# Expert stage of a graph and mixture-of-experts kernel: row-number copies on VectorE, scatter waits by loaded numbers, fetch distance of two

## What is computed

```python
gate_scores = x @ Wg + bg
_, idx = jax.lax.top_k(gate_scores, K)                    # K = 2 of E = 8 experts
mask = jax.nn.one_hot(idx, E, dtype=x.dtype).sum(axis=-2)
h = jax.nn.gelu(jnp.einsum('td,edh->teh', xf, W1) + b1[None], approximate=False)   # 256 -> 512
y = jnp.einsum('teh,ehd->ted', h, W2) + b2[None]                                     # 512 -> 256
out = jnp.einsum('ted,te->td', y, mf)
```

## Time and profile before

| | us |
|---|---|
| median of 3 runs | 177.0 (176.54 to 177.05) |
| profiled execution, its own time | 177.12 |
| its span in the trace | 175.3 |
| PE busy | 143.2 (82% of the span) |
| POOL busy | 74.8 (43%) |
| DVE busy | 89.3 (51%) |
| ACT busy | 65.3 (37%) |
| granted TensorE clock, mean | 0.989 of full speed |

### The profile page before, as it was taken

One profiled execution on the slowest core, in us unless ns is written; L12 is line 12 of the kernel. 1 busy time (PEld: TensorE's weight loads), 2 busy tenths in 40 slices (PEclk: granted clock), 3 DMA queues, 4 the chain that ended last, 5 costly groups with the idle time before them and its releaser, 6 DMA issues.

```text
span 175.3 us, 3032 instructions
## 1 busy us (share of the span) xinstructions
PE 143.2 (82%) x971; PEld 120.1 (69%) x972; DVE 89.3 (51%) x235; ACT 65.3 (37%) x183; POOL 74.8 (43%) x99
## 2 busy tenths in 40 slices
PE   1353384999999999989999948989999999999710
PEld 1332272998899899979999936857666666766600
DVE  6689999778799650305036885622222222223100
ACT  8333876467312140315030480323443333334200
POOL 6804930000499049950000200075555666663662
PEclk9999999999999999999999999999999999999995
DMA  4629999990000789400000432014244333332332
GB/s 146 194 28 310 369 366 366 368 316 12 6 0 4 204 299 327 142 4 0 0 0 4 134 128 97 0 60 90 30 71 79 64 62 60 60 64 30 60 60 30
DMA packets 16055, 20.33 MB, mean 116 GB/s; under 512 B 1754, under 2 KB 12388, under 8 KB 15908
## 3 DMA queue, kind: packets, MB, share of 16 engines
q1 hardware_dynamic: 13492, 16.54, 29.0%
q0 software_dynamic: 2544, 3.54, 12.0%
HBM read 16.81 MB, written 3.26 MB: 115 GB/s over the span
## 4 chain that ended last, share of the span: by engine, by line
PE 63%; DMA 11%; DVE 11%; issue 5%; POOL 3%; ACT 2%; POOLq 1%; SPq 1%; ACTq 0%; DVEq 0%
PE cnt_ps L1658 9%; PE bank L1639 6%; PE bank L1509 6%; DMA x_sb<-in_x 5%; PE cnt_ps L1509 4%; PE g_ps L1639 4%; PE g_ps L1344 3%; PE g_ps L1345 3%; PE g_ps L1346 3%; PE cnt_ps L1652 3%; DMA out_rows<-y_sb,row_put 2%; DMA out_rows<-y_sb,row_of 2%; DVE hot_lo L971 2%; PE cnt_ps L1344 2%; DMA xg<-x_rows,row_of 2%
## 5 line engine op out<-in xcount | busy, mean ns | idle before, releaser
L1658 PE MATMUL cnt_ps<-w_sb,h_t 128*128 x104 | 24.7, 380 | 1.1 <-ACT h_t L886 1.1
L1658 PEld LDWEIGHTS cnt_ps<-w_sb,h_t 128*128 128x128 f32 x104 | 18.8, 190 | 3.8 <-issue 1.8
L652 POOL DMA_INDIRECT out_rows<-y_sb,row_of x10 | 15.9, 1591 | 12.5 <-DMA out_rows<-y_sb,row_of 9.9
L646 POOL DMA_INDIRECT xg<-x_rows,row_of x12 | 12.1, 1005 | 18.6 <-DVE row_of L1313 15.2
L1400 PE MATMUL bank<-hot_key,hot_lo 125*128 125x45 bf16 (+4 forms) x80 | 8.3, 243 | 11.6 <-DVE hot_key L974 7.5
L1400 PEld LDWEIGHTS bank<-hot_key,hot_lo 125*128 125x128 bf16 x80 | 5.3, 123 | 13.9 <-DVE hot_key L974 13.0
L971 DVE TENSOR_TENSOR hot_lo<-iota_lo,edge_rel 125x1024 bf16<-125x1024 int16 x20 | 13.9, 697 | 1.6 <-PE g_ps L1400 1.5
L1282 DVE TENSOR_TENSOR y_sb<-cnt_ps,b_bc 128x256 f32<-128x256 f32 x13 | 5.5, 424 | 17.6 <-PE cnt_ps L1658 17.6
L1639 PE MATMUL bank<-w_sb,xt 128*128 x28 | 13.4, 600 | 0.7 <-ACT xt L890 0.5
L1278 DVE TENSOR_TENSOR h_pre<-bank,b_bc 128x512 f32<-128x512 f32 x7 | 4.8, 692 | 13.8 <-PE bank L1639 13.8
L882 ACT ACTIVATE h_act<-h_pre 128x512 f32<-128x512 f32 x13 | 8.2, 630 | 9.3 <-DVE h_pre L1278 9.3
(11 more groups left out here) (299 smaller groups left out, 405.0 us busy)
## 6 DMA issues: line engine op xcount, KB each, us to landing
w_sb<-in_L_ffn_W SPq DMA_DIRECT2D x16, 512.0 KB, 10.2
b_bc<-in_L_ffn_b SPq DMA_DIRECT2D x8, 256.0 KB, 4.8
w_stage<-in_L_gnn_W SPq DMA_DIRECT2D x3, 512.0 KB, 6.2
w_stage<-in_L_gnn_Wf SPq DMA_DIRECT2D x4, 256.0 KB, 7.5
b_bc<-in_L_ffn_b SPq DMA_DIRECT2D x1, 1024.0 KB, 8.4
x_rows<-x_f SPq DMA_DIRECT2D x1, 640.0 KB, 3.3
x_sb<-in_x SPq DMA_DIRECT2D x1, 512.0 KB
out_rows<-x_sb SPq DMA_DIRECT2D x1, 512.0 KB
```

The lines of the kernel that those rows point to most:

```text
L646: pool.indirect_dma_start(out=xg[:, b, :], out_offset=None, in_=x2_rows, in_offset=bass.IndirectOffsetOnAxis(ap=rows, axis=0)).then_inc(x_ ...
L652: pool.indirect_dma_start(out=out, out_offset=bass.IndirectOffsetOnAxis(ap=rows, axis=0), in_=y_sb[:, b, :], in_offset=None, compute_op=AL ...
L1658: last = pe.matmul(bank[3][:, 0:D], h_t[:, k, :], w2_sb[:, ds(e, 1), k, :], start=k == 0, stop=k == HC - 1)
```

## The change

- `AHEAD` is 4 instead of 5: POOL gathers two tiles instead of three before the first scatter, and in step s the tile s + 4, which PE consumes in its step s + 2. Step 9 now has a gather too (tile 13).
- `scattered` becomes two semaphores, for even and for odd tiles. Scatter s waits for its own parity (scatter s - 2 landed) and for the other parity up to a number. That number counts scatter s - 1 in if the two tiles have different experts, and leaves it out if they have the same one: an expert's tiles hold different nodes.
- DVE works the numbers out (`same_expert`, `turn_i`), and POOL loads seven of them into registers before the first gather, for tiles 3 to 9; each late tile loads its own. Tiles 1 and 2 wait for constants.
- `row_put` and `row_get` are copied by DVE, ahead of the late tile's `add_b2`, and no longer by POOL.
- SP, at the end, waits for two semaphores instead of one.

```diff
-AHEAD = 5
+AHEAD = 4
@@ gpsimd
+            pool.iota(turn_base[:].rearrange("p (k h) -> p k h", h=2), pattern=[[16, SLOT_TILES // 2], [16, 2]], base=0,
+                      channel_multiplier=0, **small).then_inc(turn_base_ready, 1)
+            pool.wait_ge(turn_ready, 1)
+            turns = [other_turn(pool, v) for v in range(3, FIXED)]
             pool.wait_ge(rows_ready, 1)
             pool.wait_ge(x2_stored, 32)
...
             for s in range(FIXED):
-                if s:
-                    pool.wait_ge(scattered, s * 16)
+                if s >= 2:
+                    pool.wait_ge(scattered[s % 2], s // 2 * 16)
+                if s in (1, 2):
+                    pool.wait_ge(scattered[1 - s % 2], 16)
+                elif s:
+                    pool.wait_ge(scattered[1 - s % 2], turns[s - 3])
                 pool.wait_ge(y_ready, s + 1)
-                scatter(s % 4, row_of[:, s:s + 1])
+                scatter(s % 2, s % 4, row_of[:, s:s + 1])
                 if AHEAD + s < FIXED + 4:
...
+            def late_scatter(s, h, n_late, n_pairs):
+                turn = other_turn(pool, s)
                 pool.wait_ge(put_taken, n_late)
                 pool.wait_ge(y_ready, s + 1)
-                pool.wait_ge(scattered, s * 16)
+                pool.wait_ge(scattered[h], n_pairs * 16 + FIXED // 2 * 16)
+                pool.wait_ge(scattered[1 - h], turn)
                 pool.sem_inc(pool_turn, 1)
...
-                    next_put(s + 1, 1 - h)
-                    pool.wait_ge(x_t_done, s + 1)
-                    pool.tensor_copy(row_get[:, h:h + 1], row_of[:, ds(s + 4, 1)]).then_inc(get_taken, 1)
@@ vector
+            dve.tensor_tensor(same_expert[:, 1:], owner[:, 1:SLOT_TILES], owner[:, 0:SLOT_TILES - 1], ALU.is_equal)\
+                .then_inc(same_ready, 1)
+            dve.wait_ge(turn_base_ready, 1)
+            dve.wait_ge(same_ready, 1)
+            dve.scalar_tensor_tensor(turn_i[:, 1:], same_expert[:, 1:], -16.0, turn_base[:, 1:], ALU.mult, ALU.add)\
+                .then_inc(turn_ready, 1)
...
-                    dve.wait_ge(scattered, s * 16 - 16)
+                    dve.wait_ge(scattered[h], p * 16 + FIXED // 2 * 16)
+                    dve.tensor_copy(row_put[:, h:h + 1], row_of[:, ds(s, 1)]).then_inc(put_taken, 1)
+                    dve.wait_ge(x_t_done, s + 1)
+                    dve.tensor_copy(row_get[:, h:h + 1], row_of[:, ds(s + 4, 1)]).then_inc(get_taken, 1)
                     add_b2(s, 2 + h, e_down)
```

More of the change, by code:

```diff
@@ L231, in build @@
         pairs_i = sb("pairs_i", [1, 2], i32, ffn)
+        turn_base = sb("turn_base", [1, SLOT_TILES], f32, ffn)
+        same_expert = sb("same_expert", [1, SLOT_TILES], f32, ffn)
+        turn_i = sb("turn_i", [1, SLOT_TILES], i32, ffn)
         iota_p = sb("iota_p", [P, P], f32, ffn)
@@ L350, in build @@
         x_t_done = sem("x_t_done")
-        scattered = sem("scattered")
+        scattered = [sem(f"scattered{h}") for h in range(2)]
+        turn_base_ready = sem("turn_base_ready")
+        same_ready = sem("same_ready")
+        turn_ready = sem("turn_ready")
         xt_ready = sem("xt_ready")
@@ L419, in up_bank, with other_turn @@
             return (bank[1], g_ps[0])[s % 2]
+        def other_turn(eng, s):
+            return eng.value_load(turn_i[0:1, ds(s, 1)], min_val=16, max_val=16 * SLOT_TILES)
         def expert_of(eng, s):
@@ L519, in _ @@
                 sp.wait_ge(x_got[h], more * 16 + 16)
-            sp.wait_ge(scattered, more * 32 + is_odd * 16 + FIXED * 16)
+            sp.wait_ge(scattered[0], more * 16 + is_odd * 16 + FIXED // 2 * 16)
+            sp.sem_inc(all_scattered, 1)
+            sp.wait_ge(scattered[1], more * 16 + FIXED // 2 * 16)
             sp.sem_inc(all_scattered, 1)
@@ L648, in gather, with scatter @@
                     in_offset=bass.IndirectOffsetOnAxis(ap=rows, axis=0)).then_inc(x_got[b], 16)
-            def scatter(b, rows):
+            def scatter(h, b, rows):
                 pool.indirect_dma_start(
                     out=out, out_offset=bass.IndirectOffsetOnAxis(ap=rows, axis=0),
-                    in_=y_sb[:, b, :], in_offset=None, compute_op=ALU.add).then_inc(scattered, 16)
+                    in_=y_sb[:, b, :], in_offset=None, compute_op=ALU.add).then_inc(scattered[h], 16)
             for s in range(2, AHEAD):
@@ L668, in _ @@
             is_odd = odd_tile(pool)
-            def next_put(s, h):
-                pool.tensor_copy(row_put[:, h:h + 1], row_of[:, ds(s, 1)]).then_inc(put_taken, 1)
-            def late_scatter(s, h, n_late):
+            def late_scatter(s, h, n_late, n_pairs):
+                turn = other_turn(pool, s)
                 pool.wait_ge(put_taken, n_late)
                 pool.wait_ge(y_ready, s + 1)
-                pool.wait_ge(scattered, s * 16)
+                pool.wait_ge(scattered[h], n_pairs * 16 + FIXED // 2 * 16)
+                pool.wait_ge(scattered[1 - h], turn)
                 pool.sem_inc(pool_turn, 1)
-                scatter(2 + h, row_put[:, h:h + 1])
-            pool.tensor_copy(row_put[:, 0:1], row_of[:, FIXED:FIXED + 1]).then_inc(put_taken, 1)
+                scatter(h, 2 + h, row_put[:, h:h + 1])
             with pool.Fori(0, more) as p:
@@ L684, in _ @@
                     s = p * 2 + (FIXED + h)
-                    late_scatter(s, h, p * 2 + (h + 1))
-                    next_put(s + 1, 1 - h)
-                    pool.wait_ge(x_t_done, s + 1)
-                    pool.tensor_copy(row_get[:, h:h + 1], row_of[:, ds(s + 4, 1)]).then_inc(get_taken, 1)
+                    late_scatter(s, h, p * 2 + (h + 1), p)
                     pool.wait_ge(get_taken, p * 2 + (h + 1))
@@ L692, in _ @@
             with pool.If(is_odd > 0):
-                late_scatter(more * 2 + FIXED, 0, more * 2 + 1)
+                late_scatter(more * 2 + FIXED, 0, more * 2 + 1, more)
         @block.scalar
@@ L1320, in _ @@
                 if s >= 4:
-                    dve.wait_ge(scattered, 16 * (s - 3))
+                    dve.wait_ge(scattered[s % 2], 16 * (s // 2 - 1))
                 add_b2(s, s % 4, e_of[s])
@@ L1334, in _ @@
                 s = more * 2 + FIXED
-                dve.wait_ge(scattered, s * 16 - 16)
+                dve.wait_ge(scattered[0], more * 16 + FIXED // 2 * 16)
+                dve.tensor_copy(row_put[:, 0:1], row_of[:, ds(s, 1)]).then_inc(put_taken, 1)
                 add_b2(s, 2, expert_of(dve, s))
```

## The result

The changed kernel takes 179.91 us (median of five executions, 178.01 to 182.86), the kernel before 177.05 in the same comparison: a ratio of 1.0129, with a 95% interval from 1.0085 to 1.0172. The ratio is taken over executions within 1.5% of the fastest of their kernel; it is not the quotient of the two medians. It is slower, as forecast, but 1.9 us above the predicted 178.0 and 1.1 us outside the range. Four of those five executions had a mean granted clock of 0.955 to 0.967, at which before takes some 2 us more as well (the table under c2_after); compared again on two chips, the change read 1.0100 (1.0046 to 1.0155) and 1.0088 (1.0048 to 1.0128).

The account below looks back on a forecast made before the run. The prediction took gapless PE (steps 1 to 9) as the bound, with scatters bound by y and late ones by landings. PE's 1.76 us delay minus 0.80 gained at the end gave +0.96, so 178.0 us; range 176.4 to 178.8.

Parts of the forecast that it names:

- X(s): Start on PE of the transposes of fetched rows in step s, those of tile s + 2; X(11) predicted 1.76 us late.
- T(12): Start on POOL of scatter 12, the last; predicted at 171.18 us against 170.22 before.
- the prediction's own recurrence: Step-by-step starts on PE and POOL, each the later of normal pace (4.10 us a step) and landing or fetch bound.
- The landing wait costs 0.8 us where it stands ahead of the scatter.: POOL, fixed part, where the expert changes: the wait costs 0.80 us instead of under 0.4.
- The rival by which it stays cheap: POOL's landing wait costs no more ahead of the scatter than inside it; 176.4 us, chance 0.17.
- Its size: At expert changes, scatter follows scatter by at least 3.74 + 0.80 = 4.54 us on POOL, against a step of 4.10.
- the sum: Whole kernel: PE 1.76 us late, less 0.80 gained at the end, net +0.96 us; profiled execution 178.1.
- the upper end that the prediction itself worked out, +1.6: Same steps with fetch issue-to-landing time 2.9 us and scatter delay 0.84 give +1.6 us.
- The stalls by the shorter distance: PE waits for fetches 0.3 to 0.5 us in steps 4, 5, 8 and 11, none in step 6.
- The gain at the end: Late scatters 10 and 11 skip the wait for the one before; with PE as before, scatter 12 starts 0.80 us earlier.
- Copies, numbers and loads at nothing: DVE's row copies and number instructions and POOL's seven loads (4.9 us) fit in idle time, costing nothing.
- from the sum to the median: Profiled 177.12 becomes 178.1; standing 0.1 above the median of 177.0, it makes the median 178.0.

Follow-up runs that it names:

- c2_after: The changed kernel repeated with no edit, on another chip than its first repeat: 178.47 us, ratio to before 1.0088.
- c1_after: The changed kernel measured again with no edit, beside the kernel before as control: 178.36 us, ratio to before 1.0100.
- f2: Changed kernel with constants for the seven loaded numbers, and the scatter itself holding the wait for the other parity: 178.86 us, ratio to before 1.0101.
- f3: Changed kernel with constants for the seven loaded numbers, waits in the order of the change: 178.66 us, ratio to before 1.0115.
- e1: Changed kernel with the old fetch distance put back (AHEAD = 5): 176.24 us, ratio to before 0.9945.
- e3: Changed kernel with the old fetch distance put back (AHEAD = 5), repeated on another chip: 177.10 us, ratio to before 0.9952.
- f1: Changed kernel with PE's loop count and late expert numbers loaded at the start of the expert part: 180.49 us, ratio to before 1.0189.
- e2: Kernel before with only the shorter fetch distance (AHEAD = 4): 180.47 us, ratio to before 1.0208.
- h1: Changed kernel with constants, the other-parity wait held by the scatter, and PE's late numbers loaded early: 179.88 us, ratio to before 1.0154.
- g1_all_wait: Changed kernel with AHEAD = 5 and numbers that let no scatter pass the one before it: 181.72 us, ratio to before 1.0315.

## Why the prediction was right in its steps and wrong in its number

X(s) - X(1) and T(12) - X(1) as predicted, in the three traces of the changed kernel, and by the prediction's own recurrence with the two sizes measured afterwards:

| | X(3) | X(4) | X(5) | X(6) | X(7) | X(8) | X(9) | X(10) | X(11) | T(12) |
|---|---|---|---|---|---|---|---|---|---|---|
| predicted | 8.23 | 12.77 | 17.31 | 21.41 | 25.61 | 30.15 | 34.25 | 38.45 | 42.99 | 51.09 |
| after | 8.25 | 12.74 | 17.35 | 21.52 | 25.74 | 30.25 | 34.41 | 39.20 | 43.30 | 51.41 |
| c1_after | 8.20 | 12.85 | 17.42 | 21.58 | 25.75 | 30.41 | 34.57 | 39.28 | 43.44 | 51.72 |
| c2_after | 8.29 | 12.86 | 17.76 | 21.92 | 26.20 | 30.78 | 34.94 | 39.65 | 43.77 | 51.99 |
| with 4.58 and 4.76 | 8.25 | 12.83 | 17.41 | 21.51 | 25.73 | 30.31 | 34.41 | 38.63 | 43.21 | 51.35 |

- **The landing wait costs 0.8 us where it stands ahead of the scatter.** Right: 0.75 in the chain, and f2 against f3 shows that it is the place. The rival by which it stays cheap falls. The Trainium skill (page "DMA: Bandwidth & Descriptors", section "Anatomy of one DMA — SWDGE (gpsimd) path") gives a dispatch of about 50 ns. If that were all that a wait moved ahead adds, scatters 2 and 3 would come 0.05 us later in f3 than in f2, measured from the scatter before; they come 0.45 and 0.36 later.
- **Its size.** From landing to landing the prediction took 4.54. The ten gaps at changes of expert that a landing ended in after and c1 are 4.48 to 4.69, mean 4.58 (scatter 5 was released by y in both); and the bound of X(s + 2) is T(s) + 4.76 to 4.77 in steps 3 to 5 of after, not 4.74. Through the chain 0.04 and 0.02 become 43.21 instead of 42.99. The recurrence then gives +1.22 us for the expert part, where the first two traces show 51.41 - 50.13 = 1.28 and 51.72 - 50.20 = 1.52. The third, c2_after, shows 51.99 - 50.20 = 1.79: there such gaps are 4.59 to 4.68, and the fetch that goes out in step 3 took 3.08 us from issue to landing, where the prediction had 2.75. Predicted was +0.96. This is the mis-sized term of the sum, 0.3 to 0.8 us; the upper end that the prediction itself worked out, +1.6, holds the first two and not the third.
- **The stalls by the shorter distance.** Right in place (steps 4, 5, 8; none in 6) and cause (e1, e3: none without it). In step 11 the wait did not show, since step 10 was late by another cause, which the prediction left out: PE's register loads for the loop, moved under the fetch wait by the distance. f1 shows that in this kernel they hide behind the fetch bound; in e2, without it, they cost 1.2 us. With the landing wait held and the loads early (h1) the shorter distance still costs X(11) 0.48 us, where the prediction, for the cheap wait, took 0.2.
- **The gain at the end.** Right: -0.79 (after) and -0.62 (c1) for -0.80.
- **Copies, numbers and loads at nothing.** Right. DVE copies in 0.14 us each, with idle time left ahead of y:

```profile
159.78 0.14 DVE L1355 COPY row_put<-row_of 128x1 int32 x1
159.84 0.14 DVE L1357 COPY row_get<-row_of 128x1 int32 x1
161.11 0.42 DVE L1305 TENSOR_TENSOR y_sb<-cnt_ps,b_bc 128x256 f32<-128x256 f32 x1 [1.13 <-PE cnt_ps L1685]
```

The seven loads were done 2.9 us ahead of the first gather, and it follows `row_of` by 0.30 as before. They took 4.1 us (106.8 to 110.9), not 4.9; the group of all ten is

```profile
L429 POOLq TENSOR_LOAD <-turn_i x10: 283/294/504, 106.8 to 167.1; - x10
```

The floor of about 600 ns that the Trainium skill gives for such a load (page "DMA: Bandwidth & Descriptors", section "Latency and other measured facts") is not what this trace shows: all ten are below it, nine at about half.

- **The step that failed: from the sum to the median.** "The profiled execution of before, 177.12, becomes 178.1; it stands 0.1 above the median of 177.0, which becomes 178.0." The sum, by the measured sizes 178.3 to 178.6 (178.8 by the trace of c2_after), is near the changed kernel at the full clock (178.41, 12 executions), and both lie inside the range. What it became as a median took for granted that the executions to be timed would have the clock of the profiled one of before, 0.989. They had 0.955 to 0.972, and neither the sum nor the range had a term for that. By the table of clocks such executions of before are themselves 2.2 us up (179.26 against 177.07). So of the 2.9 us between the medians some 1.3 are the change, by that table, and the rest goes with the clock of these executions; that is read from executions sorted by clock, as nothing here sets the clock. Why four of five executions had it, when 3 of 19 had it later, is open; the order of five numbers may be chance.

## What to carry to other kernels

Where an indirect DMA on POOL has several waits, see to it that the DMA itself holds the one that comes last: ahead of it the same wait cost 0.75 to 0.88 us here, held 0.30 (a gather) to about 0.4 (a scatter). A prefetch distance covers more than data: it also decides when an engine's in-order queue gets past its wait, and so whether the register loads behind it are free. Before a stall is put down to one cause, look for the bound right beside it; two that end at the same place give nothing back when only one is removed.

## What the runs showed of the hardware

- **The granted clock.** Executions of one program differ by stretches at the lower of TensorE's two levels (1.2 instead of 2.4 GHz), in these traces ahead of the steps that the tables compare (118 to 156 us is at 1.00 in every one). The clock also falls at the end of every trace, when PE has no work left, which costs nothing but lies in the mean: g1_all_wait has its 0.977 by that alone. Before and after, the windows 98.0 to 101.6 and 101.6 to 105.1 us (busy PE, PEld, DVE, ACT, POOL, then the granted clock):

```profile
98.00:101.60 3.60, 3.04 (x42) 2.87 (x39) 2.93 (x29) 1.60 (x5) 0.95 (x7) 1.00 0.56 174
101.60:105.10 3.50, 1.69 (x28) 1.55 (x29) 2.91 (x15) 2.94 (x5) 0.00 (x0) 1.00 0.40 141
```

```profile
98.00:101.60 3.60, 2.23 (x40) 2.05 (x40) 3.09 (x27) 2.23 (x5) 0.10 (x1) 1.00 0.43 134
101.60:105.10 3.50, 3.18 (x27) 2.95 (x24) 3.04 (x17) 1.83 (x3) 0.00 (x0) 0.51 0.65 227
```

  In after PE had been busy 2.23 of 3.60 us when the clock fell, in before 3.04, and it did not fall. c1_after, the same program, kept the full clock there, so it isn't the program that decides it; g1_all_wait had 2.22 in that window and kept the full clock too. In the profiled execution of c2_after such a stretch lasted all of the ten microseconds ahead of the fetches, and X(1) was 124.60 instead of 119.56:

```profile
105.10:115.00 9.90, 9.32 (x31) 7.00 (x32) 4.21 (x23) 0.37 (x1) 0.00 (x0) 0.51 0.20 67
```

- **A load that varies.** Of PE's five loads of an expert's number one took 620 ns, one 363 and the others 309 to 310 (e2_before_ahead4, above); on POOL the first took 504.
- **The input's landing.** The first work on x by DVE (`stats`) started at 11.34 to 11.50 us in the three traces of the kernel before and its variant, and at 10.80 to 11.08 in eight of ten of the changed kernel and its variants, at 11.38 and 11.53 in the other two. In the trace of after X(1) stands 0.43 us earlier than before (119.66 against 120.09), which makes up for the 0.3 us that the sum is short: its 178.01 against the 178.1 of the sum is two differences that cancel. Nothing in the change touches that transfer, and its cause is open; it may also be why e1 and e3 are faster at the full clock (1.36 us) than their expert part (0.7). The changed kernel should then cost less at the full clock than its expert part says, and by 1.34 us against 1.28, 1.52 and 1.79 in its three traces that is neither borne out nor refuted.
